# The sum of squares of the keys: from a VectorE reduction to ScalarE's accumulator

## The chip, the cores and the metric

The kernel runs on one core of one Trainium2 chip. The metric is the time of one execution on the device, in microseconds (us); a kernel's time is the median of its runs. The core has five engines that run side by side and wait for each other by semaphores: TensorE (PE in the profile; its weight loads are PEld), VectorE (DVE), ScalarE (ACT), GpSimd (POOL) and SyncE (SP), which issues most of the DMA transfers.

## The reference, cut to what matters

Two decoder-like layers over x of shape (8, 256, 512): cross-attention, a quantised feed-forward network, a second cross-attention with normed queries and keys, and a mixture of experts. The change is in how the keys of the second attention are prepared:

```python
NH, NKV, HD = 16, 4, 128
def _rmsnorm(x, w, eps=1e-06):
    xf = x.astype(jnp.float32)
    var = jnp.mean(xf * xf, axis=-1, keepdims=True)
    return (xf * jax.lax.rsqrt(var + eps)).astype(x.dtype) * w
k = (encoder_hidden_states @ Wk + bk).reshape(b, se, NKV, HD).transpose(0, 2, 1, 3)
v = (encoder_hidden_states @ Wv + bv).reshape(b, se, NKV, HD).transpose(0, 2, 1, 3)
k = _rmsnorm(k, kn_w)
```

The keys of a token are 512 numbers, in four groups of 128. Each group is divided by the root of the mean of its own squares.

## The kernel before

The kernel is one program of several phases with a barrier of all engines between them. The phase in question is `keys_values_ternary`, between about 306 and 416 us. It does two things side by side.

It computes keys and values of the second attention, in 16 tiles (T = 16) of 128 tokens. For each tile TensorE forms a 128x512 product of keys and one of values, each as 4 x 3 matmuls, because every float32 operand is split into a high and a low part (`matmul3`, L78 to L80). ScalarE writes the high part of the tile's context (`context_hi`, L813) and GpSimd the low part (`context_lo`, L785), three tiles ahead.

It rounds the feed-forward network's weights to -1, 0 and 1, in 24 chunks of 128x1024. A chunk comes in by DMA, ScalarE scales it (`scaled`, L835), and VectorE subtracts and clips it in two instructions (`ternary`, L897 and L899, the second on bf16 in place).

Each engine has its order written out by hand and never leaves it. In tile t:

- VectorE: `biased(t)` (L873, keys product plus bias, into `kf`), `values_out(t - 1)` (L891, into `kv_vst`), `summed(t)` (L877, sum of squares of each group, into `ksum`), one `ternary`, `normed(t)` (L881 the reciprocal, L883 the product), a second `ternary`. Tile 0 has one `ternary`, at its end. In tile 12 the four norms of the next phase stand in place of the second; tiles 13 and 14 have its maxima and scales there.
- ScalarE: `squares(t)` (L818, the squares of `kf`, into `ksq`), the first `scaled`, `root(t)` (L822, from `ksum`, into `krms`), `keys_out(t - 2)` (L829), the second `scaled`, `context_hi(t + 3)`. In tile 0 the one `scaled` stands at the end. Tile 12 has only a first `scaled`, tiles 13 to 15 have none.
- TensorE: `keys(t)`, `transposed(t - 2)` (L987), `values(t)`. Its `values(t)` waits for VectorE's value output of two tiles earlier, as there are two banks for it. TensorE runs about one tile ahead of VectorE.

`ksq` has a second use: `normed` writes the normed keys into the same buffer, from where they are transposed. `kf`, `ksq` and the banks are double-buffered.

Of the kernel before, what the change touches and what calls it, by code (L numbers as in the profile page):

```python
# [6 lines left out]
ALU = mybir.AluOpType  # L7
ACT = mybir.ActivationFunctionType
AX = mybir.AxisListType
# [19 lines left out]
def after(engine, semaphore, count):  # L29

    if count > 0:
        engine.wait_ge(semaphore, count)
# [653 lines left out]
def keys_values_ternary(nc, banks, X, eps, ident, ahead, keep, kv, prep, stored, W, rstd, f_dram, bias_dram, ctxT_dram, bk_dram,  # L686
# [12 lines left out]
    with Phase(nc) as ctx:  # L699
        def sem(name):  # L700
            return ctx.semaphore("kv_" + name)
# [3 lines left out]
        kf = [mem.take(f"kv_kf{j}", [P, G, HD]) for j in range(2)]  # L705
        ksq = [mem.take(f"kv_ksq{j}", [P, G, HD]) for j in range(2)]
# [11 lines left out]
        ksum, krms, rk = (sb(n, [P, T, G]) for n in ("ksum", "krms", "rk"))  # L718
# [5 lines left out]
        s_const, s_small, s_wn = sem("constants"), sem("small_loaded"), sem("norm_weight")  # L724
        s_c = [sem(f"ctxT{j}_loaded") for j in range(2)]
        s_chi, s_clo = sem("ctxT_hi"), sem("ctxT_lo")
        s_k, s_kf, s_ksq, s_ksum, s_krms, s_rk, s_kn, s_kt, s_kev = (sem(n) for n in (
            "k_product", "k_biased", "k_squared", "k_summed", "k_rms", "k_rrms", "k_normed", "k_transposed", "k_staged"))
        s_v, s_vf = sem("v_product"), sem("v_staged")
        s_ring = [sem(f"ring{j}_loaded") for j in range(RING)]  # L730
        s_sc, s_min, s_done = sem("scaled"), sem("min"), sem("ternary")
# [73 lines left out]
        @block.scalar  # L805
        def _(act):
            def context_hi(t):
                b = t // QT
                act.wait_ge(s_c[b % 2], (b // 2 + b % 2) * 16)
                if t >= 3:  # L810
                    act.wait_ge(s_v, t - 2)
                src = cTraw[b % 2][:, :, t % QT * P:(t % QT + 1) * P]
                act.activation(cT[t % 3].hi[:], src, ACT.Copy).then_inc(s_chi, 1)  # L813

            def squares(t):
                act.wait_ge(s_kf, t + 1)
                after(act, s_kt, max(t - 1, 0))
                act.activation(ksq[t % 2][:], kf[t % 2][:], ACT.Square).then_inc(s_ksq, 1)  # L818

            def root(t):  # L820
                act.wait_ge(s_ksum, t + 1)
                act.activation(krms[:, t, :], ksum[:, t, :], ACT.Sqrt, bias=eps_rms[:], scale=1.0 / HD).then_inc(s_krms, 1)  # L822

            def keys_out(t):
                b = t // QT
                act.wait_ge(s_kt, t + 1)
                if b >= 2:
                    act.wait_ge(stored[b % 2], b // 2 * 32)
                act.activation(kst[:, b % 2, :, t % QT * P:(t % QT + 1) * P],  # L829
                               ktb[t % 2][:].rearrange("p (g s) -> p g s", g=G), ACT.Copy, scale=wn[:]).then_inc(s_kev, 1)  # L830

            def scaled(n):
                act.wait_ge(s_ring[n % RING], n // RING * 16 + 16)
                w = n // NCH
                act.activation(ring[n % RING][:], ring[n % RING][:], ACT.Identity, bias=magic[:],  # L835
                               scale=rgamma[:, w:w + 1]).then_inc(s_sc, 1)

            def round_x(t):
                act.wait_ge(s_sx, 1)
                act.activation(prep.xn[:, t, :], prep.xn[:, t, :], ACT.Identity, bias=magic[:],  # L840
                               scale=prep.sx[:, t:t + 1]).then_inc(s_xr, 1)

            context_hi(READY)
            act.wait_ge(s_const, 1)
            for t in range(T):
                cs = rounded.get(t, range(0))
                squares(t)
                if t:
                    for n in cs[0:1]:
                        scaled(n)  # L850
                root(t)
                if t == 0:
                    act.wait_ge(s_mv, QT)
                    act.activation(std[:], mv[:, :, 1], ACT.Sqrt, bias=eps[:]).then_inc(s_std, 1)
                if t >= 2:
                    keys_out(t - 2)
                for n in cs[1:2]:
                    scaled(n)
                if t + 3 < T:
                    context_hi(t + 3)  # L860
                if t == 0:
                    scaled(0)
            round_x(0)
            round_x(1)
            keys_out(T - 2)
            keys_out(T - 1)

        @block.vector
        def _(dve):
            def biased(t):  # L870
                dve.wait_ge(s_k, t + 1)
                after(dve, s_ksq, max(t - 1, 0))
                dve.tensor_tensor(kf[t % 2][:].rearrange("p g n -> p (g n)"), kb[t % 2][:], bk[:], ALU.add).then_inc(s_kf, 1)  # L873

            def summed(t):
                dve.wait_ge(s_ksq, t + 1)
                dve.tensor_reduce(ksum[:, t, :], ksq[t % 2][:], AX.X, ALU.add).then_inc(s_ksum, 1)  # L877

            def normed(t):
                dve.wait_ge(s_krms, t + 1)  # L880
                dve.reciprocal(rk[:, t, :], krms[:, t, :]).then_inc(s_rk, 1)  # L881
                dve.wait_ge(s_rk, t + 1)
                dve.tensor_tensor(ksq[t % 2][:], kf[t % 2][:], rk[:, t, :].unsqueeze(2).broadcast_to([P, G, HD]),  # L883
                                  ALU.mult).then_inc(s_kn, 1)

            def values_out(t):
                b = t // QT
                dve.wait_ge(s_v, t + 1)
                if b >= 2:
                    dve.wait_ge(stored[b % 2], b // 2 * 32)  # L890
                dve.tensor_tensor(vst[:, b % 2, t % QT, :], vb[t % 2][:], bv[:], ALU.add).then_inc(s_vf, 1)  # L891

            def ternary(n):
                w, c = n // NCH, n % NCH
                out = flat[w][:, c * CH:(c + 1) * CH]
                dve.wait_ge(s_sc, n + 1)
                dve.tensor_scalar(out, ring[n % RING][:], ROUND, 1.0, ALU.subtract, ALU.min).then_inc(s_min, 1)  # L897
                dve.wait_ge(s_min, n + 1)
                dve.tensor_scalar(out, out, -1.0, None, ALU.max).then_inc(s_done, 1)  # L899
# [8 lines left out]
            def norm(t):  # L908
                dve.tensor_scalar(prep.xn[:, t, :], X[:, t, :], mv[:, t, 0:1], rstd[:, t:t + 1], ALU.subtract,
                                  ALU.mult).then_inc(s_xn, 1)  # L910

            def largest():
                dve.wait_ge(s_xn, PREP)
                dve.tensor_reduce(prep.ax[:, 0:PREP], prep.xn[:, 0:PREP, :], AX.X, ALU.max,
                                  apply_absolute_value=True).then_inc(s_ax, 1)
# [29 lines left out]
            for t in range(T):  # L945
                cs = rounded.get(t, range(0))
                biased(t)
                if t >= 1:
                    values_out(t - 1)
                summed(t)  # L950
                if t:
                    for n in cs[0:1]:
                        ternary(n)
                normed(t)
                for n in cs[1:2]:
                    ternary(n)
                if t == 0:
                    dve.wait_ge(s_std, 1)
                    dve.reciprocal(rstd[:], std[:]).then_inc(s_rstd, 1)
                    ternary(0)  # L960
                if t == T - 4:
                    dve.wait_ge(s_rstd, 1)
                    for j in range(PREP):
                        norm(j)
                if t == T - 3:
                    largest()
                if t == T - 2:
                    scales()
# [1836 lines left out]
def program(nc, a, out, stop=4):  # L2805
    B, S, _ = a["x"].shape
    T = B * S // P
    with ExitStack() as ctx:
# [26 lines left out]
        with Phase(nc) as cx:  # L2835
# [30 lines left out]
                       ktile(a["ctxT"]), [ktile(a[n]) for n in ("wqT", "wkT", "wvT", "woT")], B, S, ahead, ktile(a["Wk"]),  # L2866
                       ktile(a["Wv"]), weights, a["gb"])
            keys_values_ternary(nc, banks, X, eps, ident, ahead, keep, kv, prep, stored, W, rstd, weights,
                                [a[n] for n in ("gb", "vb", "ob")], ktile(a["ctxT"]), a["bk"], a["bv"], a["qn"], a["kn"], k_dram,
                                v_dram, B, S, G)  # L2870
# [79 lines left out]
```

## Time and profile before

| | |
|---|---|
| time, median of 3 runs | 1797.34 us (1795.54 to 1804.4) |
| time of the profiled execution | 1796.16 us |
| its span in the trace | 1794.4 us |
| TensorE busy / its weight loads | 1708.2 us (95%) / 1392.6 us (78%) |
| VectorE busy | 1237.1 us (69%) |
| ScalarE busy | 925.6 us (52%) |
| GpSimd busy | 593.6 us (33%) |
| L877, the sum that is removed | 16 times, 685 to 687 ns |
| L818, the squares as they are | 16 times, 629 to 632 ns |

All durations in the trace come from the one profiled execution. Busy times are sums over the whole span. Starts are in us from the span's start. An engine's idle time in square brackets, with an arrow, names what ended it. Durations of instructions on one engine may overlap by some tens of nanoseconds, since the next is started while the last one is written out.

### The profile page before, as it was taken

What the parts mean: (1) busy time and instruction counts of PE and PEld (TensorE: products, weight loads), DVE (VectorE), ACT (ScalarE), POOL (GpSimd) and SP (SyncE); (2) the same over time, 40 slices, a digit from 0 to 9 for tenths busy, and PEclk for the clock granted to TensorE, in tenths of its full rate; (3) what the DMA queues carried; (4) which work ended last, traced back from release to release, by engine and by line L of the source; (5) the groups of instructions that cost most, each with busy time, mean ns of one, the idle gap of its engine ahead of it and who ended that gap; (6) DMA issues with size and microseconds to landing.
All of it is one profiled execution on the core that took longest, in us unless ns stands there. A gap on an engine that the chain in (4) does not pass through costs nothing. (4 is left out here: it accounts for less than half of the span.)

```text
span 1794.4 us, 26446 instructions
## 1 busy us (share of the span) xinstructions
PE 1708.2 (95%) x9562; PEld 1392.6 (78%) x9582; DVE 1237.1 (69%) x2313; ACT 925.6 (52%) x1774; POOL 593.6 (33%) x469
## 2 busy tenths in 40 slices
PE   7999998996999979999999999999799999999998
PEld 6998997773444558888888788888577799999876
DVE  5444442896888768887888788888547567677555
ACT  4433432654565576676666666666231355656411
POOL 3111143223687531222231222121210255555342
PEclk9999999998999999999999999999899999999999
DMA  8223211853233671123222212210251579798573
GB/s 316 95 83 106 71 49 39 301 202 104 59 71 94 164 227 60 60 87 102 89 62 87 83 60 83 68 52 1 77 221 49 175 258 294 254 306 259 189 244 111
DMA packets 175566, 238.27 MB, mean 133 GB/s; under 512 B 51271, under 2 KB 112455, under 8 KB 173255
## 3 DMA queue, kind: packets, MB, share of 16 engines
q1 hardware_dynamic: 156620, 203.14, 34.5%
q0 software_dynamic: 9600, 33.30, 5.9%
q8 instruction: 78, 1.28, 0.3%
q10 hardware_dynamic: 9216, 0.14, 0.3%
q14 instruction: 52, 0.42, 0.1%
HBM read 184.24 MB, written 43.78 MB: 127 GB/s over the span
## 5 line engine op out<-in xcount | busy, mean ns | idle before, releaser
L1233 POOL TENSOR_TENSOR a_rq<-a_ssq,a_qhalf 128x4 f32<-128x4 f32 x64 | 65.3, 1021 | 360.4 <-DMA a_ssq<-a_sum_row 360.4
L78 PE MATMUL bank<-a_xT_hi,a_wq_lo 128*128 128x512 f32 (+1 forms) x384 | 143.3, 373 | 1.4 <-DVE a_xT_lo L503 1.4
L80 PE MATMUL bank<-a_xT_hi,a_wq_hi 128*128 128x512 f32 (+1 forms) x384 | 138.1, 360 | 0.0
L79 PE MATMUL bank<-a_xT_lo,a_wq_hi 128*128 128x512 f32 (+1 forms) x384 | 137.4, 358 | 0.0
L78 PE MATMUL bank<-a_wo_hi,a_oT_lo 128*128 128x512 f32 x320 | 127.4, 398 | 7.5 <-issue 2.7
L1396 ACT ACTIVATE a_scores<-a_scores,a_nmax 128x256 f32<-128x256 f32 x256 | 126.9, 512 | 0.8 <-DVE a_nmax L1571 0.8
L79 PE MATMUL bank<-a_wo_lo,a_oT_hi 128*128 128x512 f32 x320 | 126.4, 395 | 0.0
L80 PE MATMUL bank<-a_wo_hi,a_oT_hi 128*128 128x512 f32 x320 | 126.3, 395 | 0.0
L2111 POOL TENSOR_TENSOR e_wg_lo<-raw_g,e_wg_hi 128x1408 fp32r<-128x1408 f32 x25 | 87.9, 3514 | 112.4 <-ACT e_wg_hi L2183 112.4
L1385 ACT ACTIVATE a_sum_row<-bank,a_sum_eps 1x512 f32<-1x512 f32 x64 | 43.4, 678 | 141.0 <-PE bank L1759 140.6
L1273 POOL TENSOR_TENSOR f_h<-f_vv,f_gs 128x512 f32<-128x512 f32 x64 | 93.2, 1460 | 61.7 <-DVE f_vv L1501 61.0
L78 PE MATMUL bank<-a_pT_hi,a_V_lo 128*128 128x256 f32 x384 | 108.8, 283 | 1.4 <-DVE a_pT_lo L544 1.4
L80 PE MATMUL bank<-a_pT_hi,a_V_hi 128*128 128x256 f32 x384 | 108.7, 283 | 0.0
L79 PE MATMUL bank<-a_pT_lo,a_V_hi 128*128 128x256 f32 x384 | 108.4, 282 | 0.0
L1564 DVE SCALAR_TENSOR_TENSOR a_scores<-bank,a_rq,a_mask 128x256 f32<-128x256 f32 x256 | 105.9, 477 | 2.3 <-POOL a_rq L1233 2.3
L1585 DVE TENSOR_TENSOR a_pT_lo<-bank,a_pT_hi 128x512 fp32r<-128x512 f32 x128 | 82.0, 681 | 1.3 <-ACT a_pT_hi L1402 1.3
L80 PEld LDWEIGHTS bank<-a_xT_hi,a_wq_hi 128*128 128x128 f32 x384 | 73.0, 190 | 11.3
L78 PEld LDWEIGHTS bank<-a_pT_hi,a_V_lo 128*128 128x128 f32 x384 | 73.1, 190 | 10.9 <-issue 4.9
L78 PEld LDWEIGHTS bank<-a_xT_hi,a_wq_lo 128*128 128x128 f32 x384 | 73.5, 191 | 10.3 <-DVE a_xT_lo L503 1.8
L1571 DVE TENSOR_REDUCE a_nmax<-a_scores 128x2 f32<-128x512 f32 x128 | 81.4, 678 | 0.0
L79 PEld LDWEIGHTS bank<-a_xT_lo,a_wq_hi 128*128 128x128 f32 x384 | 73.4, 191 | 9.0
L78 PEld LDWEIGHTS bank<-a_wo_hi,a_oT_lo 128*128 128x128 f32 x320 | 60.8, 190 | 22.0 <-POOL a_wo_lo L1246 4.0
(423 smaller groups left out, 5402.3 us busy)
## 6 DMA issues: line engine op xcount, KB each, us to landing
raw_g<-in_egw SPq DMA_DIRECT2D x26, 704.0 KB, 4.7
raw_u<-in_euw SPq DMA_DIRECT2D x26, 704.0 KB, 6.2
a_xT_hi<-x1T_hi SPq DMA_DIRECT2D x16, 1024.0 KB, 6.2
a_xT_lo<-x1T_lo SPq DMA_DIRECT2D x16, 1024.0 KB, 8.4
raw_d<-in_edw SPq DMA_DIRECT2D x26, 512.0 KB, 5.8
y_routed<-m_y SPq DMA_DIRECT2D x39, 256.0 KB, 6.3
raw_d<-in_edw SPq DMA_DIRECT2D x26, 192.0 KB, 7.0
a_cTraw<-in_ctxT SPq DMA_DIRECT2D x8, 512.0 KB, 5.6
```

What stands on the lines that cost most here:

```text
L78: pe.matmul(out, w[1], x[0], start=first, stop=False)
L79: pe.matmul(out, w[0], x[1], start=False, stop=False)
L80: return pe.matmul(out, w[0], x[0], start=False, stop=last)
L1233: pool.tensor_tensor(rq[:, h % HG, :], ssq[u % 2][:], qhalf[:], ALU.pow).then_inc(s_rq, 1)
L1273: pool.tensor_tensor(h[n % 2][:, j * 512:(j + 1) * 512], vv[u % 2][:], gs[u % 2][:], ALU.mult).then_inc(s_h, 1)
L1385: act.activation(sum_row[0:1, :].rearrange("a (p t) -> a p t", t=CT), ssb[0:1, :].rearrange("a (t p) -> a p t", t=CT), ACT.Identity, bias= ...
L1396: act.activation(row, row, ACT.Exp, bias=nmax[:, i % 2, t:t + 1], accum_out=den[:, i % 2, t:t + 1]).then_inc(s_exp, 1)
L1564: dve.scalar_tensor_tensor(sc[i % 2][:, r, :], scb[b][:, t * S:(t + 1) * S], rq[:, i % HG, r:r + 1], mask[:, t, :], ALU.mult, ALU.add).the ...
L1571: dve.tensor_reduce(nmax[:, i % 2, b * QT:(b + 1) * QT], sc[i % 2][:, b * QT:(b + 1) * QT, :], AX.X, ALU.max, negate=True).then_inc(s_nmax, 1)
L1585: dve.tensor_tensor(pT[b].lo[:], ptb[b][:].rearrange("p (k s) -> p k s", k=QT), f32(pT[b].hi[:]), ALU.subtract).then_inc(ft.lo, 1)
L2111: pool.tensor_tensor(pairs[w % 2].g.lo[:], raws[raw_of(w)].g[:], f32(pairs[w % 2].g.hi[:]), ALU.subtract).then_inc(s_glo, 1)
```

## The change

ScalarE can sum what an ACTIVATE puts out, along each partition, and write the sum out (`accum_out`). It yields one sum for an instruction. There are four groups in a tile, so the one ACTIVATE of 128x512 becomes four of 128x128, each with its own sum. Each sum is written out by an instruction of its own, an ACTIVATION_READ_ACCUMULATOR in the trace. VectorE's `summed` and its semaphore go. `root` now waits for the four squares of its tile; they are ScalarE's own. The semaphore of the squares counts four a tile in place of one, and `biased` waits for four times the number.

```diff
--- before.py
+++ after.py
@@ -724,8 +724,8 @@
         s_const, s_small, s_wn = sem("constants"), sem("small_loaded"), sem("norm_weight")
         s_c = [sem(f"ctxT{j}_loaded") for j in range(2)]
         s_chi, s_clo = sem("ctxT_hi"), sem("ctxT_lo")
-        s_k, s_kf, s_ksq, s_ksum, s_krms, s_rk, s_kn, s_kt, s_kev = (sem(n) for n in (
-            "k_product", "k_biased", "k_squared", "k_summed", "k_rms", "k_rrms", "k_normed", "k_transposed", "k_staged"))
+        s_k, s_kf, s_ksq, s_krms, s_rk, s_kn, s_kt, s_kev = (sem(n) for n in (
+            "k_product", "k_biased", "k_squared", "k_rms", "k_rrms", "k_normed", "k_transposed", "k_staged"))
         s_v, s_vf = sem("v_product"), sem("v_staged")
         s_ring = [sem(f"ring{j}_loaded") for j in range(RING)]
         s_sc, s_min, s_done = sem("scaled"), sem("min"), sem("ternary")
@@ -815,10 +815,12 @@
             def squares(t):
                 act.wait_ge(s_kf, t + 1)
                 after(act, s_kt, max(t - 1, 0))
-                act.activation(ksq[t % 2][:], kf[t % 2][:], ACT.Square).then_inc(s_ksq, 1)
+                for g in range(G):
+                    act.activation(ksq[t % 2][:, g, :], kf[t % 2][:, g, :], ACT.Square,
+                                   accum_out=ksum[:, t, g:g + 1]).then_inc(s_ksq, 1)
 
             def root(t):
-                act.wait_ge(s_ksum, t + 1)
+                act.wait_ge(s_ksq, (t + 1) * G)
                 act.activation(krms[:, t, :], ksum[:, t, :], ACT.Sqrt, bias=eps_rms[:], scale=1.0 / HD).then_inc(s_krms, 1)
 
             def keys_out(t):
@@ -869,12 +871,8 @@
         def _(dve):
             def biased(t):
                 dve.wait_ge(s_k, t + 1)
-                after(dve, s_ksq, max(t - 1, 0))
+                after(dve, s_ksq, max(t - 1, 0) * G)
                 dve.tensor_tensor(kf[t % 2][:].rearrange("p g n -> p (g n)"), kb[t % 2][:], bk[:], ALU.add).then_inc(s_kf, 1)
-
-            def summed(t):
-                dve.wait_ge(s_ksq, t + 1)
-                dve.tensor_reduce(ksum[:, t, :], ksq[t % 2][:], AX.X, ALU.add).then_inc(s_ksum, 1)
 
             def normed(t):
                 dve.wait_ge(s_krms, t + 1)
@@ -947,7 +945,6 @@
                 biased(t)
                 if t >= 1:
                     values_out(t - 1)
-                summed(t)
                 if t:
                     for n in cs[0:1]:
                         ternary(n)
```

## Rows read from the trace of the kernel before

**Rows 1.** The page's first part: busy us (share of span) xinstructions.

```profile
PE 1708.2 (95%) x9562; PEld 1392.6 (78%) x9582; DVE 1237.1 (69%) x2313; ACT 925.6 (52%) x1774; POOL 593.6 (33%) x469
```

**Rows 2.** Windows: length, busy us of each engine, granted clock, DMA share, GB/s.

```profile
290.00:300.00 10.00, 7.87 (x58) 7.46 (x58) 3.73 (x9) 1.25 (x3) 0.39 (x1) 1.00 0.00 0
339.26:345.72 6.46, 6.19 (x30) 4.93 (x29) 5.81 (x10) 4.18 (x6) 2.60 (x3) 1.00 0.80 298
```

**Rows 3.** Waits, 326 to 391 us: us in total, times, longest.

```profile
PE bank L78 <- DVE kv_vst L891: 2.3, 8, 0.3
DVE f_wv L897 <- ACT kv_ring L835: 1.8, 4, 0.5
```

**Rows 4.** Timeline of VectorE: start, us, instruction, idle before it and releaser.

```profile
339.26 0.68 DVE L873 TENSOR_TENSOR kv_kf<-bank,kv_bk 128x512 f32<-128x512 f32 x1
339.86 0.68 DVE L891 TENSOR_TENSOR kv_vst<-bank,kv_bv 128x512 f32<-128x512 f32 x1
340.64 0.69 DVE L877 TENSOR_REDUCE kv_ksum<-kv_ksq 128x4 f32<-128x512 f32 x1
341.77 0.69 DVE L897 TENSOR_SCALAR f_wg<-kv_ring 128x1024 bf16<-128x1024 f32 x1 [0.45 <-ACT kv_ring L835]
342.50 0.43 DVE L899 TENSOR_SCALAR f_wg<-f_wg 128x1024 bf16<-128x1024 bf16 x1
...
344.39 1.41 DVE L899 TENSOR_SCALAR f_wv<-f_wv 128x1024 bf16<-128x1024 bf16 x1
345.72 0.68 DVE L873 TENSOR_TENSOR kv_kf<-bank,kv_bk 128x512 f32<-128x512 f32 x1
...
390.99 0.68 DVE L873 TENSOR_TENSOR kv_kf<-bank,kv_bk 128x512 f32<-128x512 f32 x1
```

**Rows 5.** Timeline of ScalarE, the same tile.

```profile
339.97 0.63 ACT L818 ACTIVATE kv_ksq<-kv_kf 128x512 f32<-128x512 f32 x1 [2.29 <-DVE kv_kf L873]
340.51 1.23 ACT L835 ACTIVATE kv_ring<-kv_ring,f_magic,kv_rgamma 128x1024 f32<-128x1024 f32 x1
341.64 0.28 ACT L822 ACTIVATE kv_krms<-kv_ksum,kv_eps_rms 128x4 f32<-128x4 f32 x1
...
342.40 1.23 ACT L835 ACTIVATE kv_ring<-kv_ring,f_magic,kv_rgamma 128x1024 f32<-128x1024 f32 x1
343.54 0.62 ACT L813 ACTIVATE kv_cT_hi<-kv_cTraw 128x512 fp32r<-128x512 f32 x1
```

**Rows 6.** Timeline of GpSimd, the same tile.

```profile
344.24 1.28 POOL L785 TENSOR_TENSOR kv_cT_lo<-kv_cTraw,kv_cT_hi 128x512 fp32r<-128x512 f32 x1 [3.65 <-ACT kv_cT_hi L813]
```

**Rows 7.** Timeline of ScalarE in the softmax, two neighbouring pairs.

```profile
904.03 0.52 ACT L1396 ACTIVATE a_scores<-a_scores,a_nmax 128x256 f32<-128x256 f32 x1
904.43 0.21 ACT L1396 ACTIVATION_READ_ACCUMULATOR a_scores<-a_scores,a_nmax 128x1 f32 x1
904.52 0.52 ACT L1396 ACTIVATE a_scores<-a_scores,a_nmax 128x256 f32<-128x256 f32 x1
```

**Rows 8.** Groups by shape, ScalarE: count, busy us, mean ns, idle before.

```profile
L835 ACT ACTIVATE kv_ring<-kv_ring,f_magic,kv_rgamma 128x1024 f32<-128x1024 f32 x24 | 29.5, 1231 | 0.0
...
L403 ACT ACTIVATE a_wraw<-a_wraw 128x1024 f32<-128x1024 f32 x24 | 25.4, 1058 | 0.0
...
L818 ACT ACTIVATE kv_ksq<-kv_kf 128x512 f32<-128x512 f32 x16 | 10.1, 630 | 39.7 <-DVE kv_kf L873 39.7
...
L2264 ACT ACTIVATE r_ex<-r_logits 128x128 f32<-128x128 f32 x1 | 0.3, 310 | 2.7 <-DVE r_logits L2390 2.7
```

**Rows 9.** Timeline of ScalarE, tile 0 and tile 13.

```profile
314.61 0.63 ACT L818 ACTIVATE kv_ksq<-kv_kf 128x512 f32<-128x512 f32 x1 [2.14 <-DVE kv_kf L873]
315.26 1.28 ACT L822 ACT_TABLE_LOAD   x1
...
398.90 0.63 ACT L818 ACTIVATE kv_ksq<-kv_kf 128x512 f32<-128x512 f32 x1 [4.16 <-DVE kv_kf L873]
400.29 0.30 ACT L822 ACTIVATE kv_krms<-kv_ksum,kv_eps_rms 128x4 f32<-128x4 f32 x1 [0.75 <-DVE kv_ksum L877]
```

**Rows 10.** Timeline of VectorE, tile 13.

```profile
400.62 0.18 DVE L881 RECIPROCAL kv_rk<-kv_krms 128x4 f32<-128x4 f32 x1 [0.37 <-ACT kv_krms L822]
```

## The prediction

> **What bounds the kernel now.** I read the page first: TensorE is busy for 95% of the span [rows 1]. That is an average over many stages, and the change lies in one of them, so I went to that stage, the key and value projection between about 306 and 416 us. The windows give one of its tiles, from 339.26 to 345.72 us [rows 2]: TensorE is busy for 6.19 of 6.46 us, VectorE for 5.81, ScalarE for 4.18. Busy shares alone can't say who sets the pace here, so the waits come next [rows 3]. TensorE waits in this stage for VectorE's value output (L891), 0.3 us at a time. VectorE waits for only one thing, ScalarE's scaled weight chunk (L835), up to 0.5 us at a time, and never for a product of TensorE. So TensorE follows VectorE, and VectorE follows ScalarE.
>
> VectorE's and ScalarE's timelines of that tile show the ring [rows 4, 5]. `biased` starts at 339.26. `squares` starts 0.71 us later, at 339.97. The scaled chunk starts 0.54 us after that, at 340.51, since an ACTIVATE of 0.63 us overlaps the next by 0.09. VectorE's `ternary` (L897) starts at 341.77, 0.03 us after the chunk is written. The sum of squares, L877, lies at 340.64 to 341.33, *before* that wait: VectorE then idles for 0.45 us all the same. After 341.77 VectorE doesn't idle until the next `biased` at 345.72. Adding up: 0.71 + 0.54 + 1.26 + (345.72 − 341.77 = 3.95) = 6.46 us, which is the period: from 345.72 to 390.99 there are seven tiles of 6.47 us [rows 4].
>
> ScalarE's other work after the chunk (root, the second chunk, the copy of the context at 343.54) runs without a gap and releases GpSimd's subtraction at 344.24 to 345.52 [rows 5, 6]. The second L899 of the tile takes 1.41 us where the first takes 0.43 [rows 4], and ends 0.28 us after GpSimd does. So there are two branches from the chunk to the next `biased`, one in VectorE's own order and one over ScalarE and GpSimd, and the second ends last. Both start at the end of `squares`. Nothing in either depends on the sum.
>
> **What is removed.** One TENSOR_REDUCE of 0.69 us in each of 16 tiles, 11 us of VectorE's time. In tiles 0 to 12 VectorE stands waiting for a scaled chunk right behind it (13 waits, 0.45 us in the tile shown), so taking it out makes that wait longer and releases nothing. I count 0 for it. `root` stands on ScalarE behind the chunk, at 341.64, when the sum had long been written at 341.33, so it gains nothing either.
>
> **What is added.** `squares` is one ACTIVATE of 128x512 now, and becomes four of 128x128, each followed by an instruction that reads the accumulator. Before this change the stage shows no such pair, so I take it from the softmax, where L1396 is the same pair with 256 columns [rows 7]: start to start it takes 904.52 − 904.03 = 0.49 us, of which the last 0.09 is the reader's. Two corrections bring this to 128 columns without a bias from memory:
>
> - Columns: the chunk without operands, L403, takes 1058 ns for 1024 columns and the squares 630 ns for 512, so 0.836 ns per column [rows 8]. 128 fewer columns save 0.107 us.
> - Operand: L835 has a bias and a scale from memory and takes 1231 ns against the 1058 of L403 [rows 8], so some 87 ns for each. L1396 has one (its maximum), `Square` none.
>
> So 0.49 − 0.107 − 0.087 = 0.296 us for a pair. A second way agrees: the one ACTIVATE of 128x128 in the trace takes 310 ns [rows 8]; with the overlap of about 0.10 that L1396 and L818 show, and 0.09 for the reader, that is 0.30. I take 0.295. Four make 1.18 us in place of 0.54 [rows 5]: **+0.64 us** on ScalarE between `biased` and the chunk.
>
> The bounds: below, a pair can't be shorter than 0.28 (the operand's 87 ns and 10 ns more of overlap taken off), which gives +0.58. Above, if I have the operand wrong, it is 0.383, and the step is 4 x 0.383 − 0.54 = +0.99.
>
> **What of it is on the path.** All of it, in tiles 0 to 12. These are the tiles in which a scaled chunk stands behind `squares` on ScalarE (in tile 0 behind the table load, which starts when `squares` has ended [rows 9] and so moves too). Queued behind the four squares are the first chunk, `root`, `keys_out`, the second chunk and the copy of the context; who waits for them is VectorE (L897, L881) and GpSimd (L785), and over the next `biased` and value output TensorE. Both branches of the ring move by the same amount. TensorE gets 0.27 + 0.64 = 0.9 us idle per tile. A stretch with more idle than this, 290 to 300 us, 7.87 of 10 us busy, was granted the full clock (1.00, the 2.4 GHz level) [rows 2]; the loaded stage would be at about 6.19 / 7.1 = 87% busy. I count nothing for the clock.
>
> In tiles 13 to 15 no chunk follows, and the sum was on the path: `root` started 400.29 − 398.90 = 1.39 us after `squares` [rows 9], of which VectorE waited 0.37 [rows 10]. Now it is three pairs of 0.295, an ACTIVATE up to its reader (0.20), the reader (0.20) and 0.04 for the semaphore: 1.33 us. Gain 0.06 us a tile, 0.2 in all.
>
> The new waits cost nothing of their own: `root` waits for ScalarE's own readers, which ended long before in tiles 0 to 12, and `biased` waits for the squares of two tiles back.
>
> **The sum.** 13 x 0.64 − 0.2 = **+8.1 us**. What follows the stage starts behind a barrier of all engines and moves as a whole. The profiled execution took 1796.16 us (span 1794.4 and 1.8 around it), which gives 1804.3; on the median of the three runs, 1797.34, it is 1805.4. I say 1805.0. With the bounds, 13 x 0.58 and 13 x 0.99: +7.3 to +12.7 us.
>
> A change within 0.5%, 9.0 us, is about what this measurement can't tell from none. My sum is +0.45%, just inside. The border lies at 9.0 / 13 = 0.69 us per tile, a pair of 0.308 us, only 13 ns above the one I use.
>
> **The rivals.**
>
> - *The pairs don't pack* (slower). If a square can't start before the reader ahead of it has ended, a pair takes 0.20 + 0.20 = 0.40 us, and the step is 4 x 0.40 − 0.54 = +1.06; with nothing overlapped at all, 0.31 + 0.20 = 0.51 and +1.50. That is +14 to +19 us, 1811 to 1816. It decides from 0.308 us on. Against it: in L1396 the next ACTIVATE starts 0.09 us after a reader of 0.21 us began [rows 7]. But those are longer instructions, and four pairs of this size stand nowhere in the trace.
> - *Order at the shared port flips* (faster). The second L899 lasts 0.98 us longer than the first one because GpSimd's subtraction, which began at 344.24, is under way when it is issued at 344.39 [rows 4, 6]. If the new spacing let L899 go first, 11 tiles would save up to 0.98 us each, less the 0.64, about −3 us in the sum with the end tiles and tile 0: 1794. Against it: both instructions hang on the same chunk, with no edit between, so the 0.15 us between them should stay. The Trainium skill, page "SBUF — State Buffer", section "Who interferes with whom", says that a VectorE instruction in a two-port mode and a GpSimd instruction exclude each other fully and that the one issued first goes first. By that rule the 1.41 us are a matter of order, which the two durations of L899 bear out, and could be lost as easily as kept.
> - *VectorE was the limit after all* (same or a little faster). If the 0.45 us wait were a by-product and the sum's slot set the ring, the period would fall until TensorE's 6.19 us bind: 12 x −0.27 = −3 us, 1794. Rows 4 speak against it in every tile: L897 starts on the chunk and not on the sum.
> - *The clock drops* (slower). If the longer gaps cost the full clock in part of the stage, TensorE's 6.2 us of work would grow past the new 7.1 us period, and 13 tiles would give +20 us or more: 1818. Only the long gaps at the stage's ends are near a lower clock; I give it little.
>
> **How the numbers follow.** The forecast, a step of +0.58 to +0.75 a tile: 0.76. Pairs that pack badly (from 0.75 up): 0.12. Port order or VectorE as limit: 0.08. Clock: 0.04. The likeliest case alone gives 1803 to 1808 with run-to-run scatter of about 2 us on it. The range of eight in ten takes in the upper bound of the pair and scatter: 1800 to 1811. Slower by over 0.5% holds the 0.16 of the slower rivals, and of the forecast the part above 0.69 a tile, with scatter about a third of 0.76: 0.25, in all 0.41. Faster by over 0.5% would need more than the faster rivals give, save with scatter: 0.03. The rest, 0.56, is within 0.5%.
>
> **What would show it.** In the profile after: four ACTIVATEs of 128x128 of about 310 ns and four readers of 0.19 to 0.21 in each tile, 0.29 to 0.30 apart; L873 to L873 at 7.1 us in place of 6.46; VectorE's wait for the chunk, which now begins when the value output ends (340.54), at 341.77 − 340.54 + 0.64 = 1.9 us; L899 still at 1.41; TensorE's wait for L891 at 0.9; tiles 13 to 15 unchanged within 0.1. The prediction is wrong if a pair isn't 0.28 to 0.31, if the period doesn't grow by four pairs less 0.54, if L899 changes its length, or if the clock of the stage is below 1.00.

## The result and the profile after

The changed kernel takes 1807.88 us, median of 16 runs (1804.28 to 1811.38), beside 1798.6 us for the kernel before in 16 runs (1795.54 to 1804.4). The ratio is 1.0047, with an interval of 1.0037 to 1.0057, so it is slower by 8.5 us (6.7 to 10.3); the two medians lie 9.3 us apart. The profiled execution took 1807.84 us, with a span of 1806.1.

Line numbers are shifted in the changed kernel: `biased` is L875 there, the value output L889, the two instructions of `ternary` L895 and L897, `squares` L819, `root` L824 and `scaled` L837.

The windows of one tile, from one `biased` to the next (same columns as in [rows 2]):

```profile
343.18:350.30 7.12, 6.19 (x30) 4.92 (x29) 5.14 (x9) 4.83 (x13) 2.62 (x3) 1.00 0.64 228
```

The tile is 7.12 us long where it was 6.46. TensorE is busy for the same 6.19 us and VectorE for 0.67 us less, ScalarE for 0.65 more. The timeline of ScalarE in this tile, which answers to [rows 5]:

```profile
343.90 0.31 ACT L819 ACTIVATE kv_ksq<-kv_kf 128x128 f32<-128x128 f32 x1 [2.28 <-DVE kv_kf L875]
344.11 0.19 ACT L819 ACTIVATION_READ_ACCUMULATOR kv_ksq<-kv_kf 128x1 f32 x1
344.20 0.29 ACT L819 ACTIVATE kv_ksq<-kv_kf 128x128 f32<-128x128 f32 x1
344.40 0.19 ACT L819 ACTIVATION_READ_ACCUMULATOR kv_ksq<-kv_kf 128x1 f32 x1
344.50 0.29 ACT L819 ACTIVATE kv_ksq<-kv_kf 128x128 f32<-128x128 f32 x1
344.69 0.19 ACT L819 ACTIVATION_READ_ACCUMULATOR kv_ksq<-kv_kf 128x1 f32 x1
344.79 0.29 ACT L819 ACTIVATE kv_ksq<-kv_kf 128x128 f32<-128x128 f32 x1
344.99 0.19 ACT L819 ACTIVATION_READ_ACCUMULATOR kv_ksq<-kv_kf 128x1 f32 x1
345.08 1.23 ACT L837 ACTIVATE kv_ring<-kv_ring,f_magic,kv_rgamma 128x1024 f32<-128x1024 f32 x1
346.21 0.28 ACT L824 ACTIVATE kv_krms<-kv_ksum,kv_eps_rms 128x4 f32<-128x4 f32 x1
```

Four pairs stand there: they start at 343.90, 344.20, 344.50, 344.79, and the chunk starts at 345.08, so a pair takes 0.295 us and the four 1.18. A reader lasts 0.19 us, but the next square starts 0.09 us after it. VectorE's timeline of the same tile, which answers to [rows 4]:

```profile
343.18 0.68 DVE L875 TENSOR_TENSOR kv_kf<-bank,kv_bk 128x512 f32<-128x512 f32 x1
343.79 0.68 DVE L889 TENSOR_TENSOR kv_vst<-bank,kv_bv 128x512 f32<-128x512 f32 x1
346.34 0.69 DVE L895 TENSOR_SCALAR f_wg<-kv_ring 128x1024 bf16<-128x1024 f32 x1 [1.88 <-ACT kv_ring L837]
347.07 0.43 DVE L897 TENSOR_SCALAR f_wg<-f_wg 128x1024 bf16<-128x1024 bf16 x1
...
348.97 1.42 DVE L897 TENSOR_SCALAR f_wv<-f_wv 128x1024 bf16<-128x1024 bf16 x1
350.30 0.68 DVE L875 TENSOR_TENSOR kv_kf<-bank,kv_bk 128x512 f32<-128x512 f32 x1
```

The place of the sum is empty, and VectorE now waits 1.88 us for the chunk where it waited 0.45. From the chunk on, everything is as before: the second clip still lasts 1.42 us. The waits, 326 to 396 us (answering to [rows 3]):

```profile
PE bank L78 <- DVE kv_vst L889: 9.3, 10, 0.9
DVE f_wv L895 <- ACT kv_ring L837: 7.5, 4, 1.9
```

TensorE waits for VectorE's value output up to 0.9 us a tile, where it was 0.3.

The stage as a whole, from the start of the first `biased` to the start of the last value output, went from 313.83 to 413.41 us before, 99.58 us, and from 315.18 to 422.96 after, 107.78: +8.20 us. The two profiled spans differ by 11.7 us. The other 3.5 us lie outside, 1.35 ahead of the stage and 2.15 behind it, where nothing was edited; in the other profiles below the first `biased` starts anywhere from 314.17 to 317.36 and the part behind the stage from 1380.5 to 1385.1, so I take this as scatter between executions. A second profile of the changed kernel, below, gives 107.73 us for the stage. For that reason the experiments are compared by the stage in the trace first, and by the ratio second.

### The profile page after: what moved, and what is told of

Same layout as the page of the kernel before. It is cut to its first block and busy times, and to the rows that moved or that the text cites. A ratio compares the mean times of both kernels' runs of the same rounds, so it can differ in the third digit from the quotient of the medians.

```text
span 1806.1 us, 26542 instructions
## 1 busy us (share of the span) xinstructions
PE 1712.2 (95%) x9562; PEld 1395.5 (77%) x9582; DVE 1226.9 (68%) x2297; ACT 936.0 (52%) x1886; POOL 593.9 (33%) x469
## 3 DMA queue, kind: packets, MB, share of 16 engines
q8 instruction: 78, 1.28, 0.3%
## 5 line engine op out<-in xcount | busy, mean ns | idle before, releaser
L78 PEld LDWEIGHTS bank<-a_xT_hi,a_wq_lo 128*128 128x128 f32 x384 | 74.0, 193 | 10.3 <-DVE a_xT_lo L503 1.8
```

What stands on the lines that cost most here:

```text
L78: pe.matmul(out, w[1], x[0], start=first, stop=False)
```

## The experiments

The question was no longer the sign but whether the price is where the prediction put it: in the ring from `biased` over `squares` to the chunk. For each run the table gives the starts of `biased` of tiles 1 and 12 on VectorE's timeline, the mean period between them (a difference over 11), the stage from the start of the first `biased` to the start of the last value output, and the ratio of times to the kernel before with its interval.

| kernel | tile 1, tile 12 | period | stage | ratio |
|---|---|---|---|---|
| before | 319.88, 390.99 | 6.46 | 99.58 | |
| changed | 321.87, 400.12 | 7.11 | 107.78 | 1.0047 (1.0037 to 1.0057) |
| changed, again | 323.25, 401.46 | 7.11 | 107.73 | 1.0051 (1.0034 to 1.0069) |
| no sum | 323.41, 394.48 | 6.46 | 97.38 | 0.9993 (0.9982 to 1.0004) |
| split only | 321.41, 395.52 | 6.74 | 103.95 | 1.0026 (1.0015 to 1.0038) |
| one reader | 322.63, 394.75 | 6.56 | 98.86 | 1.0005 (0.9991 to 1.0018) |
| short low part | 323.58, 391.03 | 6.13 | 95.97 | 0.9984 (0.9974 to 0.9994) |
| changed, chunk first | 322.23, 389.11 | 6.08 | 94.56 | 0.9979 (0.9968 to 0.9989) |
| before, chunk first | 321.59, 389.69 | 6.19 | 96.02 | 0.9989 (0.9978 to 1.0001) |
| changed, chunk first and context early | 323.97, 387.85 | 5.81 | 91.57 | 0.9962 (0.9947 to 0.9976) |
| before, chunk first and context early | 320.21, 386.62 | 6.04 | 94.33 | 0.9977 (0.9967 to 0.9986) |

**Half the change alone: no sum.** On the kernel before:

```diff
-                act.wait_ge(s_ksum, t + 1)
+                act.wait_ge(s_ksq, t + 1)
...
-                summed(t)
+            pool.memset(ksum[:], 1.0)
```

> The kernel before with VectorE's sum left out and nothing put in its place: squares stay one ACTIVATE of 128x512, ksum holds a constant 1, so the keys are not normalised by their own size. Ring theory (the pace is biased, squares, first scaled chunk, then both branches): the slot of the sum releases nothing while a chunk follows; the period from one biased to the next stays at 6.46 us in tiles 1 to 11, VectorE's wait for the chunk grows from 0.45 to about 1.2 us, and only tiles 13 to 15 get shorter, by about 0.73 us each, in all -2 us. Rival (VectorE was the limit): the period falls to TensorE's 6.0 to 6.2, 11 tiles x 0.3 and more, in all -5 us.

The period stays at 6.46 us to the hundredth. VectorE's timeline shows why:

```profile
349.84 0.68 DVE L892 TENSOR_TENSOR kv_vst<-bank,kv_bv 128x512 f32<-128x512 f32 x1
351.75 0.69 DVE L898 TENSOR_SCALAR f_wv<-kv_ring 128x1024 bf16<-128x1024 f32 x1 [1.23 <-ACT kv_ring L836]
```

It waits 1.23 us for the chunk in place of 0.45, and starts it when it would have started it anyway. The stage gets 2.20 us shorter, and 2.16 of it after tile 12's `biased`: from there to the last value output it is 20.26 us (394.48 to 414.74) where it was 22.42 (390.99 to 413.41). So what the change removes from VectorE is worth nothing in the ring; the gain is in the last three tiles, where no chunk follows.

**The other half: split only.** On the kernel before, four squares of 128x128, without accumulator, and VectorE's sum stays (its wait and that of `biased` count four squares a tile):

```diff
-                act.activation(ksq[t % 2][:], kf[t % 2][:], ACT.Square).then_inc(s_ksq, 1)
+                for g in range(G):
+                    act.activation(ksq[t % 2][:, g, :], kf[t % 2][:, g, :], ACT.Square).then_inc(s_ksq, 1)
...
```

> The kernel before with the squares as four ACTIVATEs of 128x128, no accumulator; VectorE still sums. Ring theory: the four start 0.20 us apart and take 0.80 in place of 0.54, so the period goes from 6.46 to 6.73 us, and with it 13 x 0.26 plus 3 x 0.26 in the end tiles, +4.2 us. Of the 0.65 us of the change, 0.26 is then the splitting and 4 x 0.093 the readers. Rival (the accumulator is the whole price): the period stays at 6.46, +0 us.

ScalarE's timeline in one tile:

```profile
349.06 0.91 ACT L819 ACTIVATE kv_ksq<-kv_kf 128x128 f32<-128x128 f32 x4 [2.28 <-DVE kv_kf L874]
349.88 1.23 ACT L836 ACTIVATE kv_ring<-kv_ring,f_magic,kv_rgamma 128x1024 f32<-128x1024 f32 x1
```

The four (merged in one line) start at 349.06 and the chunk at 349.88: 0.82 us, and the period grows by 0.27. The stage is +4.37 us. Splitting alone is thus 0.27 of the 0.65 us per tile, and the four readers are the other 0.38.

**One reader.** On the changed kernel, one square over all four groups with one sum. The groups are then scaled by a sum that isn't their own, which `root` reads four times:

```diff
-                for g in range(G):
-                    act.activation(ksq[t % 2][:, g, :], kf[t % 2][:, g, :], ACT.Square,
-                                   accum_out=ksum[:, t, g:g + 1]).then_inc(s_ksq, 1)
+                act.activation(ksq[t % 2][:], kf[t % 2][:], ACT.Square, accum_out=ksum[:, t, 0:1]).then_inc(s_ksq, 1)
...
```

> The changed kernel with one ACTIVATE of 128x512 and one accumulator read per tile; all four groups are scaled by the sum over the whole tile, so the groups are not kept apart. Ring theory: squares to chunk is 0.54 + 0.09 = 0.63 us, the period 6.56 us, +1.2 us in tiles 0 to 12, and -0.63 us in each of tiles 13 to 15, in all about -0.7 us against the kernel before. Rival (what counts is VectorE's freed time, 0.69 us a tile): a period below 6.46 and some -5 us. Rival (an accumulator costs its full 0.2 us): period 6.66, +0.7 us in all.

ScalarE's timeline in one tile:

```profile
349.56 0.63 ACT L818 ACTIVATE kv_ksq<-kv_kf 128x512 f32<-128x512 f32 x1 [2.29 <-DVE kv_kf L873]
350.10 0.19 ACT L818 ACTIVATION_READ_ACCUMULATOR kv_ksq<-kv_kf 128x1 f32 x1
350.19 1.23 ACT L835 ACTIVATE kv_ring<-kv_ring,f_magic,kv_rgamma 128x1024 f32<-128x1024 f32 x1
```

From the square to the chunk 0.63 us, as expected; the period is 6.56 and the stage −0.72 us. A reader of 0.19 us costs 0.09 in the ring. With one sum to a tile the change would have been free; with four it isn't.

**The branch over GpSimd: short low part.** On the changed kernel, GpSimd's subtraction works on 4 of 128 columns from tile 3 on; the rest of the context's low part is left stale:

```diff
-                pool.tensor_tensor(cT[t % 3].lo[:], src, f32(cT[t % 3].hi[:]), ALU.subtract).then_inc(s_clo, 1)
+                n = P if t == READY else 4
+                pool.tensor_tensor(cT[t % 3].lo[:, :, 0:n], src[:, :, 0:n], f32(cT[t % 3].hi[:, :, 0:n]),
+                                   ALU.subtract).then_inc(s_clo, 1)
```

> The changed kernel with GpSimd's subtraction of the context's low part cut to 4 of 128 columns per slice from tile 3 on, the rest of the low part left stale. Ring theory with two branches, the one over GpSimd ending last: the second bf16 clip of each tile falls from 1.41 to 0.43 us and the period from 7.11 by up to 0.98 us, to where TensorE's own work binds, 6.1 to 6.2 us, in all about -10 to -11 us against the changed kernel (about -2 against the kernel before). Rival (the 1.41 us belong to the instruction and not to GpSimd): clip and period unchanged. Rival (VectorE's branch ends last anyway): the clip falls and the period stays near 7.1.

VectorE's timeline at the end of a tile, and GpSimd's in the same place:

```profile
347.02 0.69 DVE L897 TENSOR_SCALAR f_wv<-kv_ring 128x1024 bf16<-128x1024 f32 x1
347.75 0.43 DVE L899 TENSOR_SCALAR f_wv<-f_wv 128x1024 bf16<-128x1024 bf16 x1
348.09 0.68 DVE L877 TENSOR_TENSOR kv_kf<-bank,kv_bk 128x512 f32<-128x512 f32 x1
```

```profile
347.59 0.21 POOL L786 TENSOR_TENSOR kv_cT_lo<-kv_cTraw,kv_cT_hi 128x16 fp32r<-128x16 f32 x1 [4.32 <-ACT kv_cT_hi L815]
```

The clip at 347.75 takes 0.43 us in place of 1.41: GpSimd's instruction, now 0.21 us long, ends 0.05 us after the clip starts. The next `biased` follows at once. The period is 6.13: 7.11 less the whole 0.98. So the branch over GpSimd did end last, and the 1.41 us are a wait and not the clip's own work. The Trainium skill, page "SBUF — State Buffer", section "Who interferes with whom", describes this as a lock on ports that VectorE and GpSimd share, held for a whole instruction; the two durations agree with it.

Against the changed kernel the stage is 11.81 us shorter, more than the 10 to 11 expected, as twelve periods lose the 0.98, that behind tile 12's `biased` too. The expectation also named TensorE's own work as what would bind at 6.1 to 6.2 us; the period fits, the reason doesn't, as the last pair of runs shows.

**The chunk out of the ring.** The edit is the same on both kernels, and was run on both, beside the changed kernel itself:

```diff
-                squares(t)
                 if t:
                     for n in cs[0:1]:
                         scaled(n)
+                squares(t)
                 root(t)
```

> The changed kernel once more, beside the reordered ones. Ring theory: +8.2 us against the kernel before (13 x 0.65, less 0.2), 1.0047 as a ratio, period 7.11 us.

> The changed kernel with ScalarE's first scaled chunk of each tile put ahead of the squares. Ring theory: the chunk leaves the ring, since ScalarE scales it while it waits for biased anyway; what is left is squares, root, keys_out, second chunk, context, GpSimd: about 6.11 us, and TensorE's own 6.0 to 6.2 us. The period falls from 7.11 to 6.1 to 6.2, about -11 us against the changed kernel and -3 against the kernel before. Rival (the four pairs cost time wherever they stand on ScalarE): the period stays at 6.8 or more.

> The kernel before with the same reordering: chunk first, then the one square; VectorE still sums. Ring theory: VectorE's branch has the sum in it now, the GpSimd branch comes to about 6.19 us, so the period is 6.1 to 6.2 us, -3 to -4 us against the kernel before, and equal to the changed kernel in the same order within 1.5 us. Rival (with the chunk out of the way the sum on VectorE binds): period above 6.3 us, and the changed kernel in this order is the faster one by 2 us or more.

ScalarE's timeline in the changed kernel with the chunk first; the chunk belongs to the tile whose squares follow it:

```profile
350.64 1.24 ACT L837 ACTIVATE kv_ring<-kv_ring,f_magic,kv_rgamma 128x1024 f32<-128x1024 f32 x1
353.04 0.31 ACT L819 ACTIVATE kv_ksq<-kv_kf 128x128 f32<-128x128 f32 x1 [1.17 <-DVE kv_kf L875]
...
354.36 0.30 ACT L824 ACTIVATE kv_krms<-kv_ksum,kv_eps_rms 128x4 f32<-128x4 f32 x1
```

The chunk starts at 350.64, in time in which ScalarE would have idled, and is ready 1.2 us before the squares start. The changed kernel drops from 107.73 to 94.56 us in the stage. That is 13.17 us, where some 11 were expected: the period behind tile 1's `biased` fell by 1.52 us (7.09 to 5.57) and that behind tile 12's by 1.86 (7.85 to 5.99), the ten between by 0.98 each. The four pairs are all still there, so what made the change slower was the chunk behind them. What is left is the branch over GpSimd, at 6.13 us in a usual tile, where 6.11 was expected (the table's mean of 6.08 has the short tile 1 in it).

The kernel before gains less, 3.56 us. In this order the sum on VectorE *is* on the path: `root` stands behind no chunk and waits 0.75 us for it. From `biased` to `root` it is 2.10 us there (339.90 to 342.00) and 2.03 with the change (352.33 to 354.36). So the pairs still cost their time, but what they replace now costs as much. The two kernels differ by 1.46 us of stage, at the edge of what I had expected. Run beside each other, 12 runs each, their medians are 1794.22 us with the change and 1797.07 without; the intervals of their ratios overlap. In this order the change is no longer the slower one.

**Both branches loosened.** As above, and the copy of the context moved ahead of the second chunk:

```diff
-                for n in cs[1:2]:
-                    scaled(n)
                 if t + 3 < T:
                     context_hi(t + 3)
+                for n in cs[1:2]:
+                    scaled(n)
```

> The changed kernel with the first chunk ahead of the squares, and the copy of the next context ahead of the second chunk, so that GpSimd's subtraction starts about 1.14 us earlier in the tile. Theory: after the first reordering the branch over GpSimd still sets 6.13 us (0.71 + 1.28 + 0.04 + 0.19 + 0.57 + 1.14 + 0.70 + 1.28 + 0.20 = 6.11); with the copy early that branch ends by 5.9 us, the second clip is short (0.43 us), VectorE waits for the second chunk, and TensorE's own work is left as the limit, between 5.95 and 6.13 us a tile: 0 to -2 us against the reordered kernel, -4 to -7 against the kernel before. Rival (GpSimd now meets VectorE's product of two SBUF inputs or its first clip, and one of them waits out the other): the clip moves its 0.98 us elsewhere and the period is 6.2 us or more.

> The kernel before with both reorderings, VectorE still summing. Theory: the limit is TensorE here too, the period equals that of the changed kernel in this order within 0.05 us, and the two differ only in tiles 13 to 15 and tile 0 (0.2 us for the accumulator, 0.65 against it). Rival (VectorE's sum binds once everything else is out of the way: its own instructions add up to 0.60 + 0.67 + 0.77 + 0.73 + 0.34 + 0.21 + 0.62 + 0.73 + 0.34 = 5.01 us plus its waits): period at least 0.1 us above the other's, and the changed kernel ahead by more than 1.5 us.

The changed kernel in this order, timelines of VectorE, ScalarE and GpSimd in one tile:

```profile
335.04 0.68 DVE L875 TENSOR_TENSOR kv_kf<-bank,kv_bk 128x512 f32<-128x512 f32 x1
...
337.61 0.69 DVE L881 TENSOR_TENSOR kv_ksq<-kv_kf,kv_rk 128x512 f32<-128x512 f32 x1
339.63 0.76 DVE L895 TENSOR_SCALAR f_wg<-kv_ring 128x1024 bf16<-128x1024 f32 x1 [1.33 <-ACT kv_ring L837]
340.43 0.43 DVE L897 TENSOR_SCALAR f_wg<-f_wg 128x1024 bf16<-128x1024 bf16 x1
340.77 0.68 DVE L875 TENSOR_TENSOR kv_kf<-bank,kv_bk 128x512 f32<-128x512 f32 x1
```

```profile
335.76 0.31 ACT L819 ACTIVATE kv_ksq<-kv_kf 128x128 f32<-128x128 f32 x1 [0.74 <-DVE kv_kf L875]
...
337.07 0.30 ACT L824 ACTIVATE kv_krms<-kv_ksum,kv_eps_rms 128x4 f32<-128x4 f32 x1
...
337.85 0.62 ACT L813 ACTIVATE kv_cT_hi<-kv_cTraw 128x512 fp32r<-128x512 f32 x1
338.37 2.37 ACT L837 ACTIVATE kv_ring<-kv_ring,f_magic,kv_rgamma 128x1024 f32<-128x1024 f32 x2
```

```profile
338.54 1.30 POOL L785 TENSOR_TENSOR kv_cT_lo<-kv_cTraw,kv_cT_hi 128x512 fp32r<-128x512 f32 x1 [4.43 <-ACT kv_cT_hi L813]
```

Its usual tile takes 340.77 − 335.04 = 5.73 us on VectorE. Of the eleven periods in the mean of 5.81, one takes 6.96, in which VectorE waits 1.64 us for a store of K to land, and the first takes 5.35. It is the fastest of all, 0.9962.

The 5.73 us are below the 5.95 to 6.13 that I had expected of TensorE, but TensorE doesn't do a tile in that time. The rows of TensorE where the keys of tiles 5 and 6 start, and the windows between them, with those of an early tile of the kernel before under them:

```profile
340.48 0.39 PE L78 MATMUL bank<-kv_wk_hi,kv_cT_lo 128*128 128x512 f32 x1
346.41 0.39 PE L78 MATMUL bank<-kv_wk_hi,kv_cT_lo 128*128 128x512 f32 x1
```

```profile
340.48:346.41 5.93, 5.93 (x29) 4.90 (x28) 4.48 (x9) 5.14 (x14) 2.18 (x3) 1.00 0.87 332
324.92:330.85 5.93, 5.93 (x30) 4.89 (x28) 5.28 (x10) 3.81 (x6) 1.20 (x1) 1.00 0.79 304
```

TensorE has no wait in the list of waits from 326 to 387 us and takes 5.93 us a tile, in the kernel before just as here when it is held up by nobody. VectorE, at 5.73, lives on TensorE's head start: from the first keys matmul of a tile to its `biased` it is 6.77 us in tile 7 (352.43 to 359.20) and 5.75 in tile 12 (382.10 to 387.85), 0.20 less for each tile. The stage ends before the head start is used up. With many more tiles VectorE would have to fall in with the 5.93 us; that is an estimate from these rows, no run here is that long.

The kernel before in the same order, timelines of VectorE, ScalarE and GpSimd:

```profile
350.28 0.69 DVE L873 TENSOR_TENSOR kv_kf<-bank,kv_bk 128x512 f32<-128x512 f32 x1
...
353.53 0.69 DVE L883 TENSOR_TENSOR kv_ksq<-kv_kf,kv_rk 128x512 f32<-128x512 f32 x1
354.95 0.99 DVE L897 TENSOR_SCALAR f_wv<-kv_ring 128x1024 bf16<-128x1024 f32 x1 [0.72 <-ACT kv_ring L835]
355.97 0.43 DVE L899 TENSOR_SCALAR f_wv<-f_wv 128x1024 bf16<-128x1024 bf16 x1
356.31 0.68 DVE L873 TENSOR_TENSOR kv_kf<-bank,kv_bk 128x512 f32<-128x512 f32 x1
```

```profile
352.39 0.30 ACT L822 ACTIVATE kv_krms<-kv_ksum,kv_eps_rms 128x4 f32<-128x4 f32 x1 [0.75 <-DVE kv_ksum L877]
```

```profile
353.86 1.52 POOL L785 TENSOR_TENSOR kv_cT_lo<-ahead_ctx,kv_cT_hi 128x512 fp32r<-128x512 f32 x1 [3.08 <-ACT kv_cT_hi L813]
```

Here my expectation fell and the sign of its rival held: the periods aren't equal, 6.03 against 5.73 us, and the change is ahead. But it isn't VectorE's own time that binds, though its sum is a link of the chain that does (`root` waits 0.75 us for it). GpSimd still ends last: from `biased` to the end of its subtraction it is 338.54 + 1.30 − 335.04 = 4.80 us with the change and 353.86 + 1.52 − 350.28 = 5.10 without it, and from there to the next `biased` 0.93 us in both. It is now the first instruction of the second `ternary` that GpSimd holds up: it takes 0.76 and 0.99 us where it took 0.69. So GpSimd ends last only narrowly here: ScalarE's second chunk releases the same instruction, and without GpSimd the tile would be some 0.07 and 0.30 us shorter, an estimate from these durations. The 0.30 us between them have two parts. With the sum on VectorE, `root` stands 2.11 us behind `biased` (352.39 less 350.28), with the accumulator 2.03 (337.07 less 335.04), so the subtraction starts 0.08 us later. And it then takes 1.52 us in place of 1.30. In the second kernel VectorE's product, whose two operands are both in SBUF, is under way when it starts (353.53 to 354.22 beside 353.86); in the first the product has ended (338.30 beside 338.54). That this meeting is the reason for the longer subtraction is read from timelines; no run changes it alone. The other traces speak for it. In the kernel before, the ten subtractions from 331.30 to 389.50 meet no such product and take 1.28 to 1.30 us. The next one starts 0.06 us behind a product and takes 1.78:

```profile
394.77 0.69 DVE L883 TENSOR_TENSOR kv_ksq<-kv_kf,kv_rk 128x512 f32<-128x512 f32 x1
```

```profile
394.83 1.78 POOL L785 TENSOR_TENSOR kv_cT_lo<-kv_cTraw,kv_cT_hi 128x512 fp32r<-128x512 f32 x1 [2.78 <-ACT kv_cT_hi L813]
```

With 0.63 us of the product left it takes 0.49 us longer, with 0.36 left 0.23.

## Why the prediction was right, step by step

- *The ring.* Right. `biased` to `squares` 0.71, squares to chunk, chunk to `ternary`, and the rest as before. The period grew by 0.65 us; predicted 0.64.
- *The removed sum is worth 0 in tiles 0 to 12.* Right, and shown alone: period unchanged without it.
- *The pair.* Predicted 0.295 us from the softmax's pair less columns and less the operand; measured 0.295. The upper bound of 0.383, without the operand's share, was not needed. The readers and the splitting, apart, are 0.38 and 0.27 us.
- *Two branches, both moved.* Right; that the one over GpSimd ended last was shown by taking its 0.98 us away.
- *Tiles 13 to 15.* Predicted −0.2 us in all. From tile 13's `biased` to the last value output it was 15.22 us (398.19 to 413.41) and is 14.99 (407.97 to 422.96): −0.23.
- *The sum.* Predicted +8.1, in the stage +8.20. In whole runs 8.5 with an interval of 6.7 to 10.3. The time itself, 1807.88 us, is 2.9 above the 1805.0 predicted; 1.3 of that is the median of the kernel before, which went from 1797.34 in three runs to 1798.6 in sixteen. On which side of 0.5% the change came out was luck: 0.47% with an interval of 0.37% to 0.57%, and 0.51% in the second set of runs.
- *The clock.* Nothing lost: 1.00 in the tile shown, with TensorE idle for 0.93 us of it, and 1.00 in every stretch of 10 us from 320 to 410.
- *The rivals.* Pairs that don't pack, VectorE as the limit, and a changed order at the port are all refuted, the first by the starts, the second by the run without the sum, the third by the clip of 1.42 us in the rows after.
- *What was wrong* is a side term: that TensorE's own work binds at 6.19 us a tile. I had read it off its busy time in a tile in which it also waited. When TensorE waits for nobody it does a tile in 5.93 us, in the kernel before (324.92 to 330.85) as in the last order, so the 6.19 us were no floor. The forecast didn't hang on it, but the rival "VectorE was the limit" would have been worth up to 12 x 0.53 us and not 12 x 0.27. The expectations that named TensorE as the next limit missed too: in all the orders tried VectorE's usual periods, 5.73 to 6.20 us, were set by its own chain or by GpSimd's branch, and the shortest of them drew on TensorE's head start.

## What to carry to other kernels

An accumulator isn't free on ScalarE: each sum needs an instruction of its own, and each group a start of its own. Before moving a reduction to it, look at what stands *behind* it in ScalarE's queue, and not at how busy either engine is: here VectorE was 90% busy in the tile shown and had 0.69 us a tile taken off it, for nothing, as it was waiting for the very engine that got the work. The change stops being a loss once the order of the queue is right: with both orders changed its stage is 2.76 us the shorter one. In whole runs that is less sure (medians of 1791.7 us in 6 runs and 1793.73 in 11, intervals that overlap). So fix the order first, and try the change again.

And don't read a floor off an engine's busy time in a tile in which it waits. Look for a stretch in which it waits for nobody and take its period there: 5.93 us here, not 6.19.

## What the runs showed of the hardware

- A square of 128x128 with its accumulator read takes 0.295 us back to back; the first of a row lasts 0.31 us, the others 0.29, a reader 0.19, of which 0.09 count. The Trainium skill, page "ScalarE: Activation LUTs", section "What ACT_TABLE_LOAD costs", gives 186 ns and 0.833 ns per column for an ACTIVATE without operands in memory, 293 ns here, which the trace bears out.
- Contention of VectorE and GpSimd goes both ways. A bf16 clip of 0.43 us becomes 1.41 when it comes second; a GpSimd subtraction of 1.29 us takes 1.52 when it starts with 0.36 us left of a VectorE product of two SBUF operands, and 1.78 with 0.63 left. The first is shown by a run that shortens GpSimd's instruction, the second is read from timelines only.
